# Splitting gathered rows through PSUM, half a group at a time, in a graph network's aggregation

## What is computed

```python
# layer 0: graph convolution, residual, layer norm
h = segment_sum(norm[:, None] * (x @ W)[src], dst, N) + b   # with self loops
x = layernorm(x + h + t_emb @ Wt + bt)
# layers 1 and 2: two SAGE convolutions with a relu between, residual, layer norm
def sage(x, Wl, Wr, b):
    mean = segment_sum(x[src], dst, N) / maximum(count, 1)[:, None]
    return mean @ Wl.T + x @ Wr.T + b
x = layernorm(x + sage(relu(sage(x, Wl1, Wr1, b1)), Wl2, Wr2, b2))
```

## Time and profile before

| | us |
|---|---|
| median of 3 runs | 3868.2 (3867.39 to 3877.09) |
| the profiled execution | 3877.73 |
| its span, first to last instruction | 3875.7 |
| mean granted TensorE clock in it | 0.895 of full speed |
| stage with few split groups (layer 0, 29 blocks) | 153 to 865 |
| rest of layer 0 (20 blocks) | 865 to 1355 |
| layer 1 (49 blocks) | 1397 to 2585 |
| layer 2 (49 blocks) | 2665 to 3857 |

### The profile page before, as it was taken

How to read it: one execution, slowest core, us unless ns; L and a number is a source line. 1 busy time by engine, 2 the same in 40 slices (tenths; PEclk the granted TensorE clock), 3 DMA queues, 4 the chain that set the end, 5 groups by cost and what they waited for, 6 DMA issues and landing times.

```text
span 3875.7 us, 56484 instructions
## 1 busy us (share of the span) xinstructions
PE 3103.1 (80%) x9474; PEld 1698.3 (44%) x9476; DVE 2085.1 (54%) x5736; ACT 1200.7 (31%) x1704; POOL 2418.7 (62%) x2365
## 2 busy tenths in 40 slices
PE   7367788888888878878888878878888888788787
PEld 7133333344444544444444444444444444444444
DVE  8533233345655655555555555545455555565565
ACT  0311111123434433333333333333233333343343
POOL 0366666666666566666666666646666666667664
PEclk9788888998989998989899989989889989899998
DMA  5766666666666666666666667656666666666664
GB/s 165 261 181 184 187 174 191 190 203 196 196 196 198 181 211 197 196 179 198 200 202 198 205 196 220 195 182 202 180 184 187 186 185 192 181 186 190 179 184 142
DMA packets 262343, 742.09 MB, mean 191 GB/s; under 512 B 50445, under 2 KB 52015, under 8 KB 262280
## 3 DMA queue, kind: packets, MB, share of 16 engines
q0 software_dynamic: 187680, 615.14, 54.9%
q10 hardware_dynamic: 56622, 104.45, 7.8%
q1 hardware_dynamic: 18010, 22.16, 1.8%
HBM read 688.66 MB, written 53.71 MB: 192 GB/s over the span
## 4 chain that ended last, share of the span: by engine, by line
PE 33%; issue 31%; another core or an unknown queue 9%; POOL 5%; ACTq 5%; DMA 4%; DVE 4%; ACT 4%; DVEq 4%; POOLq 0%; SPq 0%
PE sum_ps L958 20%; PE prod_ps L965 5%; PE root_ps L965 5%; POOL raw L413 5%; DMA raw<-table,idx_ring 3%; DVE raw L651 2%; ACT hi L818 2%; DVE oh L624 2%; PE aggT_ps L939 1%; DVEq L624 1%; ACT hbuf L773 1%; DMA table<-stage 1%; PE sum_ps L927 1%; ACTq L242 1%
## 5 line engine op out<-in xcount | busy, mean ns | idle before, releaser
L413 POOL DMA_INDIRECT raw<-table,idx_ring x2346 | 2409.3, 1027 | 1336.0 <-issue 759.8
L651 DVE TENSOR_TENSOR raw<-raw,hi 128x344 fp32r<-128x344 f32 x2298 | 1155.9, 509 | 1179.4 <-issue 719.5
L958 PE MATMUL sum_ps<-raw,oh 128*128 128x512 f32 x3172 | 1316.6, 539 | 14.0 <-issue 7.5
L818 ACT ACTIVATE hi<-raw 128x1024 fp32r<-128x1024 f32 x766 | 788.7, 1054 | 1139.0 <-issue 883.2
L958 PE MATMUL sum_ps<-hi,oh 128*128 128x512 f32 x1532 | 640.8, 502 | 386.6 <-issue 227.0
L624 DVE TENSOR_SCALAR oh<-iota_row,tile_base,dst_tab 128x128 fp32r<-128x128 bf16 x2358 | 794.8, 355 | 229.3 <-issue 200.4
L958 PEld LDWEIGHTS sum_ps<-raw,oh 128*128 128x128 f32 x3172 | 657.9, 209 | 413.8 <-issue 308.2
L965 PE MATMUL prod_ps<-W,aggT 128*128 128x512 f32 x1176 | 558.1, 619 | 54.8 <-issue 32.2
L958 PEld LDWEIGHTS sum_ps<-hi,oh 128*128 128x128 f32 x1532 | 280.5, 205 | 619.1 <-issue 599.6
L965 PE MATMUL root_ps<-W,selfT 128*128 128x512 f32 x800 | 428.7, 686 | 59.7 <-issue 36.0
L965 PEld LDWEIGHTS prod_ps<-W,aggT 128*128 128x128 f32 x1176 | 232.8, 200 | 327.1 <-issue 318.9
(11 more groups left out here) (128 smaller groups left out, 1207.3 us busy)
## 6 DMA issues: line engine op xcount, KB each, us to landing
selfbuf<-table ACTq DMA_DIRECT2D x152, 256.0 KB
raw<-table,idx_ring POOLq DMA_INDIRECT x2346
table<-stage ACTq DMA_DIRECT2D x7, 1792.0 KB, 6.5
table<-X ACTq DMA_DIRECT2D x49, 256.0 KB
table<-hbuf ACTq DMA_DIRECT2D x49, 256.0 KB
X<-table ACTq DMA_DIRECT2D x49, 256.0 KB
X<-in_x SPq DMA_DIRECT2D x6, 2048.0 KB
out<-X ACTq DMA_DIRECT2D x48, 256.0 KB
```

What stands on the lines that cost most here:

```text
L413: nc.gpsimd.indirect_dma_start(out=raw[:, n, j, :], out_offset=None, in_=tables[L][:, :], in_offset=bass.IndirectOffsetOnAxis(ap=idx_ring[ ...
L651: return v.tensor_tensor(low, rows, high.bitcast(fp32), ALU.subtract)
L818: a.activation(rounded(n), raw[:, n, :, :], ACT.Copy).then_inc(S["hi_ready"], 1)
L958: last = mm(bank, of[:, j, :], half[:, j, :], start=fresh, stop=False, skip_group_check=True)
```

## The change

ScalarE now rounds and shows a group in halves of 512 columns: it rounds a half into `hi`, waits until VectorE has read the same half of the split group before (or all of the group before), and writes the rounded half a second time, from `raw`, into its own PSUM bank (`high_ps`, two banks, one per half). VectorE waits for each half and subtracts `raw - high_ps`. The two banks come from the products, of which one is left (`PR` = 1). `LEAD` goes from 2 to 1 and `FIN_LAG` from 3 to 2. The counter `rows_ready` starts at one.

```diff
-    PIECES = ((0, 344), (344, 680), (680, CH * D))
...
-    PR = 3
-    LEAD = 2
-    FIN_LAG = 3
+    LEAD = 1
+    PR = 1
+    FIN_LAG = 2
...
+        high_ps = pb("high_ps", [P, CH * D], fp32)
...
-            return prod_ps[:, bass.ds((t1 % PR) * D, D)]
+            return prod_ps[:, :]
...
+            dve.sem_inc(S["low_made"], 1)
+            dve.sem_inc(S["rows_ready"], 1)
...
-                def part(n, cols):
-                    rows, high, low = (of.rearrange("p c d -> p (c d)")[:, cols[0]:cols[1]]
-                                       for of in (raw[:, n, :, :], rounded(n), lo[:, n, :, :]))
-                    return v.tensor_tensor(low, rows, high.bitcast(fp32), ALU.subtract)
+                def low_part(n, j, splits):
+                    dve.wait_ge(S["high_shown"], splits * CH + (j + 1))
+                    return v.tensor_tensor(lo[:, n, j, :], raw[:, n, j, :], high_ps[:, j * D:(j + 1) * D],
+                                           ALU.subtract)
...
                         if n in split:
-                            k = split.index(n)
-                            dve.wait_ge(S["hi_ready"], (b - first_block) * len(split) + (hi_base + k + 1))
-                            part(n, PIECES[0])
+                            splits = (b - first_block) * len(split) + (hi_base + split.index(n))
+                            low_part(n, 0, splits).then_inc(S["low_made"], 1)
                             next(following)
-                            part(n, PIECES[1])
-                            next(following)
-                            part(n, PIECES[2]).then_inc(S["rows_ready"], 1 + unsplit_next)
+                            low_part(n, 1, splits).then_inc(S["rows_ready"], 1)
+                            last = next(following)
+                            if unsplit_next:
+                                last.then_inc(S["rows_ready"], 1)
...
+                def show_high(n, j):
+                    a.activation(high_ps[:, j * D:(j + 1) * D].bitcast(f32r), raw[:, n, j, :],
+                                 ACT.Copy).then_inc(S["high_shown"], 1)
...
                             act.wait_ge(S["gathered"], b * SLOTS + (NG * L + n + 1))
-                            a.activation(rounded(n), raw[:, n, :, :], ACT.Copy).then_inc(S["hi_ready"], 1)
+                            splits = (b - first_block) * len(split) + (hi_base + split.index(n))
+                            a.activation(rounded(n)[:, 0, :], raw[:, n, 0, :], ACT.Copy)
+                            act.wait_ge(S["low_made"], splits + 1)
+                            show_high(n, 0)
+                            a.activation(rounded(n)[:, 1, :], raw[:, n, 1, :], ACT.Copy)
+                            act.wait_ge(S["rows_ready"], b * SLOTS + (NG * L + n + 1))
+                            show_high(n, 1)
...
-                        pe.wait_ge(S["rows_ready"], g + (NG * L + 1))
+                        pe.wait_ge(S["rows_ready"], g + (NG * L + 2))
```

More of the change, by code:

```diff
@@ L174, in gnn_resnorm @@
         prod_ps = pb("prod_ps", [P, PR * D], fp32)
+        high_ps = pb("high_ps", [P, CH * D], fp32)
         root_ps = pb("root_ps", [P, D], fp32)
         hist_ps = root_ps
-        tmp_ps = [prod_ps[:, n * D:(n + 1) * D] for n in range(PR)] + [sum_ps[:, 0:D]]
+        tmp_ps = [prod_ps[:, 0:D], high_ps[:, 0:D], high_ps[:, D:2 * D], sum_ps[:, 0:D]]
         names = """edges_copied pad_made dst_loaded x_loaded consts_made oh_ready oh_used hist_done deg_made
             total_ps rows_loaded rows_cast src_ps dst_ps tabs_made loads_done bias_ps b0_made b0_all_ps b1_all_ps bias_made x_biased ended_made
-            staged stage_stored0 stage_stored1 zero_stored wl_loaded wr_loaded chain rows_ready gathered hi_ready
+            staged stage_stored0 stage_stored1 zero_stored wl_loaded wr_loaded chain rows_ready gathered
             pe_done self_loaded sum_ready agg_ready aggT_done aggT_ready prod_ready prod_read next_made next_used
@@ L184, in gnn_resnorm @@
             mean_ready squares_made rstd_ready norm_ready x_stored h_stored h_ready x_reloaded idx_copied
-            out_stored ended_ps slot_claimed x_tail_zero""".split()
+            out_stored ended_ps slot_claimed x_tail_zero high_shown low_made""".split()
         names += """order_read order_ps order_known sort_loaded sort_consts sort_oh_made sort_ranked sort_placed
```

## The result

The changed kernel takes 4094.7 us (4 runs, 4066.4 to 4106.8) against 3867.8 us: a ratio of 1.057, 95% interval 1.051 to 1.064. The sign of the forecast is right; the size is not, 227 us where 70 were expected. Its profiled execution takes 4066.4 us, the fastest of the four, so the two profiles differ by 189 us only.

A forecast was written before the change was run, and what follows sets the result against it. POOL and PE were both taken as near full, neither alone the bound. Terms -60 + 90 + 15 + 25 = +70 us on the profiled 3877.7 us, forecast 3938 us against 3868.2; range 3770 to 4100 us.

The forecast's parts named there:

- The freed gathers: POOL's gathers beside the subtraction: one operand in PSUM should free POOL of 183 us.
- the single bank and `FIN_LAG` 2: Products at tile ends: one product bank and `FIN_LAG` 2 cost nothing, since PE's wait is covered by other work.
- the signs named for the profile: Changed profile: ScalarE idle before roundings under 400 us, PE's waits before split groups' first products up some 90, among others.
- The roundings: ScalarE's four half activations per split group: pitch goes from 1.79 to 2.04 us in 375 catch-up groups, +90 us.
- the tile ends: `LEAD` 1 at 147 tile ends: +35 us, less 20 us of PE's wait for `agg`, +15 us.
- a margin of 1.0 us in place of 1.9: Tile ends: PE's own work of 6.3 us against ScalarE's 5.3 before its next group; margin shrinks from 1.9 us.
- the gathers: POOL's gathers: one third credited of the 183 us freed, -60 us; ends 0 and -183.
- the new waits: ScalarE waiting for VectorE before showing a half: 0.25 us for each of 98 root rounds, +25 us; ends 0 and +200.
- the 576 us of waits for slots: POOL before its gathers: 576 us idle waiting for ring slots PE has not freed, so faster gathers may only wait longer.
- The ports' case: Rival, POOL's gathers decide: all 183 us gained give 3700 us, half 3777; chance 0.28.
- No relief: Rival: the second SBUF operand is not what delays POOL, the rest holds, 3998 us; chance 0.08.
- ScalarE as the bound: Rival: ScalarE, busy 1119 of 1188 us in layer 1, becomes the bound; 4060 us taken; chance 0.17.

The follow-up runs named there:

- k2_load: Changed kernel without ScalarE's waits for VectorE, halves shown in one bank, VectorE subtracting `hi` from SBUF in halves: 3924.6 against 3813.3 us, ratio 1.030.
- k1_relief: Kernel before with `LEAD` 1, `PR` 1, `FIN_LAG` 2, VectorE subtracting a zeroed PSUM bank in two halves: 3499.7 us, ratio 1.027; repeated 3496.9, 1.028.
- k0_base: Kernel before with only the schedule constants changed (`LEAD` 1, `PR` 1, `FIN_LAG` 2): 3467.5 against 3408.5 us, ratio 1.017.

## Why the prediction was right and wrong

**Right, and to the size.** The freed gathers (priced at 183 us of POOL's time, 174 measured); the pitch of a split group on ScalarE (2.04 us, 2.08 measured); ScalarE's total (835 us more, 857 measured); the half subtraction (0.69 us); the single bank and `FIN_LAG` 2 at nothing, in setting A (1.0005) and, by the 1.002 of the changed kernel with `LEAD` 2, in B. Of the signs named for the profile, two were missed: ScalarE idle 586 us before the first rounding of a group, where under 400 were expected, and PE's idle time before the first products of split groups up by 151 us, not 90.

**The roundings**, +90 us, with **the tile ends**, +15 us, in A. `k2_load` has all of ScalarE's load and `LEAD` 1, and is 111 us slower than the kernel before beside it; `LEAD` 1 alone has 1.001. The two terms, 105 us together, come out at their size. In B the load costs 66 us over layers 0 and 1, which have 472 of the 766 split groups; 90 us for all would be 55 for these. For the tile ends B is another matter: there `LEAD` 1 is the whole loss, 72 us on the kernel before. What I weighed, a margin of 1.0 us in place of 1.9, seems to decide in B, where PE is busy 86% of the span against 80% in A; no run takes that margin apart. (With the pitches as I gave them, 2.04 and 1.79 us, the difference is 0.25 and not 0.24 us, and the term 94 us; it changes nothing.)

**Where the sum failed: the gathers and the new waits together.** I had -60 + 25 = -35 us for them. The changed kernel less `k2_load`, which is what they are in the runs, comes to some 110 us in setting A: the forecast's first 105 us were right, and the step from there went the other way.

**The gathers**, -60 us. The direction holds where it could be measured alone. In B the relief gained 80 us over layers 0 and 1, where a third of POOL's 127 us would have been 42: the 576 us of waits for slots did not swallow it, and I credited too little. What it is worth in A was not measured. POOL's waits grew there by 363 us, but that follows from whatever else made the kernel slower.

**The new waits**, +25 us. If the relief is worth anything at all in A, what stands beside it between `k2_load` and the changed kernel costs more than 110 us, at least four times this term. The only thing that I priced there is this wait, at 0.25 us per root round. But the start of the layers, where the root rounds are dense, lost little, and the ends lost most: if the waits are the cause, they were priced at the wrong place, since behind every tile end, too, VectorE has other work (1.2 us from 2407.01 to 2408.22 in the timeline above) during which ScalarE may now not round ahead. In setting B the same waits cost nothing (1.016 with, 1.0165 without). So they are one candidate for A. The stalls in VectorE's queue are the other: they were in no term of the sum, though the trace of the kernel before had 595 of them. The cause of this half stays open.

**The rivals.** The ports' case (chance 0.28) fell as a forecast of the time, but not as a mechanism: with layer 1's 42 us (1088 to 1046 us) once more for layer 2, the gain in B would be an estimated 120 us, where this case asked for half to all of 183. "No relief" asked for an unchanged gather time and fell too; that its sum, 3998 us, was nearer is luck. ScalarE as the bound (0.17) came nearest in size, but not as told: ScalarE is busy 51% and still idle 586 us before its roundings. That 4094.7 us lies within the range of 3770 to 4100 is luck as well: the range was drawn for other reasons.

**The setting.** One more thing was behind the forecast unseen: all durations and waits came from one execution in setting A, and I took its 0.7 us queue instructions and "remote" waits for the kernel's own. I had a row of such instructions in the 6.54 us before one rounding, and put it among ScalarE's fixed costs.

## What to carry to other kernels

Do not read the worth of a relief from how an engine's waits change between two kernels of different length: POOL's grew by 363 us, and yet the relief alone, in the one setting where it was measured, brought 80 of 127 us. Compare the time at which the same piece of work is done, stage by stage. In `k1_relief` two layers had gained 80 us and the third lost 100 to something else, and the total told only the sum. When an operation is split to feed a second consumer, count the producer's pitch against the consumer's (here 2.08 against 1.79 us), and keep the producer's freedom to run ahead. And measure a schedule constant in more than one setting: `LEAD` 1 was free where the kernel took 3880 us, and cost 2.2% where it was 3406.

## What the runs showed of the hardware

The same kernel with the same inputs takes 3404 to 3409 us in one setting and 3813 to 3880 us in the other. The mark in the trace is in the queues. VectorE's sequencer instructions of one line, and the waits of ScalarE for the sums, of the kernel before with `LEAD` 1, stand here first for setting A (`b_lead1`) and then for B (`b_lead1b`). Each has a fence for the line of the queue (duration ns min/median/max) and one for the waits of the activation at line 749 (idle us and times):

```profile
L643 DVEq ALU_OP  x1176: 3/40/1437, 154.4 to 3853.6; - x196
```

```profile
  remote: 324.8, 30
```

```profile
L643 DVEq ALU_OP  x1176: 40/40/47, 154.1 to 3446.1; - x196
```

```profile
  PE sum_ps L930: 497.3, 96
  PE sum_ps L927: 248.8, 49
```

In B every such instruction takes 40 to 47 ns and every wait of this line has a known releaser; in A some take 0.7 us and more, and 30 waits end by an update that the trace can't assign. The mean granted TensorE clock is 0.92 to 0.96 in B and 0.88 to 0.91 in A, and the matmuls of this kernel are busy 2984 us in B against 3118 us in A. What makes the two settings is not known from these runs.

In layer 2 of `k1_relief`, with about five instruction-fetch packets per block, VectorE's queue stands still for 4.1 us at the head of its block loop in each of 48 blocks, against 0.24 us in layer 1, which has four such packets in all. The stops are 182 us longer in all, and the layer takes 100 us longer than in `k0_base`.

ScalarE writes 512 columns to PSUM in 0.58 us and to SBUF in 0.61 to 0.62 us, in both settings and at the same pitch of 0.52 us. A gather beside a subtraction with one operand in PSUM keeps its 0.95 us; with two in SBUF the mean over all gathers is 1.02 to 1.03 us. The Trainium skill (SBUF — State Buffer, "Who interferes with whom") has it, as an inference, that a `tensor_tensor` does not hold descriptor generation up; the mean of 1024 against 953 ns in two kernels that differ in that operand and run in the same setting (`k2_load` and the changed kernel, in A) speaks against it. So do 1034 and 950 ns in `k0_base` and `k1_relief`, in B, which differ in nothing but the subtraction; that it comes in halves is not what frees the gathers, since `k2_load` subtracts in halves too.
